# Experts with weights split ahead of time into float32r parts in DRAM, in two slots of one expert each

## The chip, the cores and the metric

The kernel runs on one core of a Trainium2 chip. The metric is the device time of one execution in microseconds (us), the median of several runs. The core has five engines that run their own instruction streams and wait for each other by semaphores: TensorE (PE; weight loads are listed as PEld), VectorE (DVE), ScalarE (ACT), GpSimd (POOL) and SyncE (SP), which here only issues transfers.

## What is computed

Two blocks of a graph network and a mixture of experts each, on 3125 nodes of 256 features and 50000 edges. The change is in the first mixture of experts (16 experts, the best two for each row), whose weights it prepares during the graph part ahead of it:

```python
x = x + L0_gnn(layernorm(x), weight[16], edge_weight, src, dst, edge_type)
x = x + L0_ffn(layernorm(x), ...)
# L0_ffn: D_MODEL 256, HIDDEN 512, 16 experts
probs = softmax(x @ gate_w + gate_b);  top_probs, top_idx = top_k(probs, 2)
hidden = silu(x @ w1[e]) * (x @ w2[e])      # 256 -> 512, for each chosen expert e
out = sum over the two chosen e of (hidden @ w3[e]) * share[e]      # 512 -> 256
x = x + L1_gnn(layernorm(x), ...);  x = x + L1_ffn(layernorm(x), ...)
```

All is float32. float32r is a form in which TensorE takes a float32 matrix product in one pass with fewer bits; a product kept near float32 is made of three such terms (high x high, high x low, low x high), where low is what the rounding to high left over.

## The kernel before

The stages run one after another, with a barrier of four engines between them.

**Transform** (lines 404 to 450). All nodes times the 16 relations' matrices: 25 row tiles, each 8 groups of six float32r products of 512 columns (L422). ScalarE copies each group's bank to the stage buffer (L434), SyncE writes it to DRAM (L439). VectorE splits the tile's rows into high and low parts, and at chosen tiles builds edge tables (`dve_tables`).

**Gather** (lines 722 to 845). 196 blocks of 256 edges. GpSimd fetches the transformed rows with 392 indirect loads (L784); before the blocks b = 8, 12, ... it waits until block b-5 has landed (`ld_ok`). TensorE multiplies each of 221 steps with a one-hot matrix from VectorE (L826) and VectorE adds the result (L835). Beside it ScalarE makes 28 pairs of one-hot tables for later (`act_places`, L740 to L755), each written to DRAM.

**Routing** (`*_routing`): norm, gate logits, the best two experts, the place of each row in a list sorted by expert. An expert has whole tiles of 128 rows; MT = 64 tiles is the most that can occur and all 64 are run. VectorE ends the routing with the place tables (`fri`, `toi`) and then with work on the next layer's weights (L1066 to L1072).

**Experts' stage** (`*_moe`), the place of the change, a loop over 64 tiles:
- SyncE (`sp_tile`) loads the three matrices of the tile's expert, 512 KB each, for every tile, into one of three buffers. The expert's number is in a register of SyncE.
- GpSimd (`rows_of_tile`) fetches the tile's 128 rows, and scatters the results (`results`).
- TensorE (`pe_moe`): turns the rows of tile j+1 (L1255, L1256), makes the two up products of tile j in plain float32 with the weights stationary (L1267; 16 products of 128x128, two instructions each), so that the hidden rows come out transposed, and the down product of tile j-1 as three float32r terms (L1279, 12 products of 256 columns).
- ScalarE copies the turned rows (L1297), rounds w3 (L1304), applies Silu (L1308), rounds the hidden rows (L1310). VectorE makes w3's low part (L1323), Silu times the second up product (L1326), the hidden rows' low part (L1328), and copies out (L1335).

The engines' order is the order of the code; there is no planner. Addresses of weights in SBUF are constants, chosen by j % 3.

## Time and profile before

| | us |
|---|---|
| median of 3 runs | 2679.85 (2675.83 to 2681.54) |
| the profiled execution | 2671.94 |
| its span | 2670.2 |
| transform, first to last product | 30.7 to 309.5 |
| gather, first to last indirect load | 315.3 to 808.8 |
| experts' stage, first up product to last down product | 901.9 to 1237.9 |
| TensorE busy in all | 1939.5 |
| GpSimd busy in all | 1398.1 |

The span is the time between the first and the last instruction of the program. An engine counts as busy while it executes; waits, register steps and the issue of transfers don't count. The end of a matrix product is modelled with its way through the array, so products in a row overlap: their rate is read from start to start. The granted clock of TensorE is given as a share of its full speed.

### The profile page before, as it was taken

To read this page: it belongs to the slowest core of one execution; us is meant where nothing else is said; L and a number is where in the kernel's file an instruction comes from. 1 tells how busy PE (TensorE), PEld (TensorE's weight loads), DVE (VectorE), ACT (ScalarE), POOL (GpSimd) and SP (SyncE) were. 2 spreads that over 40 slices of the span, in tenths; PEclk is the share of its full clock that TensorE was granted. 3 is DMA by queue.
4 is the path that set the end of the run, shared out by engine and by line. 5 is a ranking of instruction groups with operands and counts; after the bars stand their busy time and mean duration, and the time that the engine had idled before them with its cause. 6 is when DMAs were issued, how large, how long until landed. Compare 5 with 4: busy or idle time off the path is not lost.

```text
span 2670.2 us, 37572 instructions
## 1 busy us (share of the span) xinstructions
PE 1939.5 (73%) x10213; PEld 1484.5 (56%) x10213; DVE 1545.9 (58%) x4921; ACT 920.6 (34%) x2031; POOL 1398.1 (52%) x1413
## 2 busy tenths in 40 slices
PE   7999766666666699996466667675466666666798
PEld 5888644444443599996344444444344444444477
DVE  5200134334346755556468787788468787888743
ACT  4444499996002244443221111111311111112522
POOL 1100277777771244432377777771477777772233
PEclk9999878777777799998778788888778888888899
DMA  5544577776334699996455555551455555551000
GB/s 210 201 194 189 200 238 244 237 239 193 105 104 108 229 353 351 352 349 220 155 159 172 158 176 158 172 175 36 141 159 174 157 175 160 170 174 37 1 25 25
DMA packets 206433, 472.17 MB, mean 177 GB/s; under 512 B 33180, under 2 KB 99958, under 8 KB 199762
## 3 DMA queue, kind: packets, MB, share of 16 engines
q0 software_dynamic: 63424, 179.09, 23.3%
q1 hardware_dynamic: 111986, 188.65, 19.8%
q10 hardware_dynamic: 30816, 101.99, 10.7%
q8 instruction: 91, 1.49, 0.2%
q14 instruction: 116, 0.95, 0.1%
HBM read 365.49 MB, written 104.92 MB: 176 GB/s over the span
## 4 chain that ended last, share of the span: by engine, by line
PE 36%; POOL 31%; issue 14%; DVE 11%; DMA 5%; ACT 1%; DVEq 1%; POOLq 0%; SPq 0%; ACTq 0%
POOL arena L1474 18%; POOL arena L784 13%; PE banks L422 10%; PE banks L1267 9%; PE banks L1279 3%; DMA arena<-ht,srcT 3%; PE banks L1583 2%; PE banks L1584 1%; PE banks L1433 1%; DVE arena L1756 1%; PE banks L2175 1%; DVE arena L1672 1%; PE banks L2177 1%; PE banks L2176 1%; DMA arena<-tr,idx1T 1%
## 5 line engine op out<-in xcount | busy, mean ns | idle before, releaser
L1474 POOL DMA_INDIRECT arena<-ht,srcT x784 | 785.7, 1002 | 311.3 <-issue 231.6
L784 POOL DMA_INDIRECT arena<-tr,idx1T x392 | 375.3, 957 | 327.1 <-DMA tr<-arena 207.9
L812 PE MATMUL banks<-arena 128*128 x884 | 323.6, 522 | 182.5 <-SPq L791 170.8
L1583 PE MATMUL banks<-arena,XT 128*128 128x264 f32 x884 | 375.8, 515 | 103.0 <-DVE arena L1756 84.9
L812 PEld LDWEIGHTS banks<-arena 128*128 128x128 f32 x884 | 213.8, 259 | 292.3 <-issue 258.4
L1584 PE MATMUL banks<-arena,XT 128*128 128x264 f32 x884 | 335.3, 468 | 0.0
L1756 DVE TENSOR_TENSOR arena<-arena,nrmT 128x528 f32<-128x528 f32 x442 | 309.6, 703 | 20.3 <-ACT nrmT L1530 19.0
L1583 PEld LDWEIGHTS banks<-arena,XT 128*128 128x128 f32 x884 | 188.6, 241 | 201.1 <-DVE arena L1756 133.5
L422 PE MATMUL banks<-parts 128*128 128x512 f32 x1200 | 275.0, 391 | 4.7 <-DVE parts L382 4.7
L835 DVE TENSOR_TENSOR X<-X,banks 128x256 f32 x221 | 91.9, 416 | 312.4 <-PE banks L812 311.6
L422 PEld LDWEIGHTS banks<-parts 128*128 128x128 f32 x1200 | 226.0, 189 | 52.3 <-issue 5.3
L1510 ACT COPY xn<-arena 128x16 f32 x448 | 54.5, 202 | 554.9 <-SPq L791 547.5
L1584 PEld LDWEIGHTS banks<-arena,XT 128*128 128x128 f32 x884 | 213.4, 241 | 51.3
L1267 PE MATMUL banks<-arena 128*128 128x128 f32 x2048 | 240.4, 275 | 0.0
L1267 PEld LDWEIGHTS banks<-arena 128*128 128x128 f32 x2048 | 235.0, 193 | 0.0
L1541 PE MATMUL banks<-ident,xn 128*64 128x128 f32 x112 | 31.2, 375 | 269.3 <-ACT xn L1510 269.3
L1672 DVE TENSOR_TENSOR arena<-arena,banks 128x264 f32 x442 | 188.7, 427 | 13.2 <-PE banks L1584 3.2
L434 ACT COPY arena<-banks 128x512 f32<-128x512 f32 x200 | 116.8, 587 | 160.1 <-PE banks L422 155.1
L1541 PEld LDWEIGHTS banks<-ident,xn 128*64 128x64 f32 x112 | 9.6, 130 | 291.3 <-ACT xn L1510 237.0
L1156 POOL DMA_INDIRECT ys<-arena x64 | 63.9, 999 | 185.6 <-DVE arena L1335 185.6
L826 DVE TENSOR_SCALAR arena<-iorow,dlT,nrmT 128x128 f32<-128x128 f32 x442 | 137.6, 362 | 31.8 <-PE banks L422 31.8
L751 ACT ACTIVATE arena<-iorow,dlT 128x128 bf16<-128x128 f32 x448 | 133.8, 387 | 11.3 <-ACT arena L742 11.3
(370 smaller groups left out, 3033.2 us busy)
## 6 DMA issues: line engine op xcount, KB each, us to landing
arena<-in_L_ffn_w_dram SPq DMA_DIRECT2D x192, 512.0 KB, 6.1
tr<-arena SPq DMA_DIRECT2D x50, 1024.0 KB, 3.9
XT<-otd ACTq DMA_DIRECT2D x52, 512.0 KB, 4.5
...
arena<-ht,srcT POOLq DMA_INDIRECT x784, 2.9
```

The costliest lines, as they stand in the source:

```text
L422: mm = ten.matmul(B[b][:, :], x[c][:, k, :], w[:, k, 2 * j:2 * j + 2, :].rearrange("p r d -> p (r d)"), start=(n == 0), stop=(n == 5))
L434: act.copy(stage[:, i % 2, j * 512:(j + 1) * 512], B[j % 6][:, :]).then_inc(ev_ok, 1)
L751: v = ac.put(act.activation(OHs[b][:, j * P:(j + 1) * P], iorow[:, :], ACT.Abs, scale=-1.0, bias=dlT[:, q:q + 1]))
L784: pool.indirect_dma_start(Gr[:, o:o + D], None, TR, bass.IndirectOffsetOnAxis(ap=idx1T[:, q:q + 1], axis=0)).then_inc(d_g[b % NG], 16)
L812: mm = ten.matmul(B[n][:, 0:D], OHr[:, n, h, :], Gr[:, h * D:][:, bass.ds(o, D)], start=(h == 0), stop=(h == 1))
L826: vec.tensor_scalar(OHr[:, n, h, :], iorow[:, :], dlT[:, q:q + 1], nrmT[:, q:q + 1], ALU.is_equal, ALU.mult).then_inc(oh_r, 1)
L1267: mm = ten.matmul(B[bank][:, h * P:(h + 1) * P], W[b][:, k, h * P:(h + 1) * P], xTt[c][:, k, :], start=(k == 0), stop=(k == 1))
L1474: pool.indirect_dma_start(Gall[:, o:o + ROW], None, HT[L], bass.IndirectOffsetOnAxis(ap=srcT[:, q:q + 1], axis=0)).then_inc(d_g[b % NG], 16)
L1583: ten.matmul(B[n][:, 0:MSG], OH[b][:, 2 * j, :], WG[:, j, 0, :], start=True, stop=False)
L1584: mm = ten.matmul(B[n][:, 0:MSG], OH[b][:, 2 * j + 1, :], WG[:, j, 1, :], start=False, stop=True)
L1672: ins = vec.tensor_tensor(o, o, B[j % 4][:, 0:MSG], ALU.add)
L1756: vec.tensor_tensor(WG[:, j].rearrange("p a (h c) -> p a h c", c=HW), gm, ex.to_broadcast([P, 2, 8, HW]), ALU.mult).then_inc(w_ok, 1 + CH ...
```

## The change

- **Splitting.** A DRAM tensor WS holds, for each expert and each of its three matrices, the high and the low part side by side, 1 MB a matrix. 48 pieces (one matrix each) are read by ScalarE's queue, rounded by ScalarE, subtracted by VectorE and written back by ScalarE's queue: `act_piece` 15 times at the end of a row tile of the transform and once in each of the 28 iterations of `act_places`, the rest behind it; `dve_piece` in step with it, in the gather at fixed steps (`low_at`).
- **Slots.** Two slots in SBUF of one expert each (three matrices, high and low, 3 MB). SyncE loads expert 0 at the start of the routing, expert 1 when the places are known, and expert e into slot e % 2 matrix by matrix as soon as the last tile of expert e-2 has used that matrix. Every expert is loaded once, in the order of their numbers.
- **Up products.** Now with the turned rows stationary and the weights moving: six float32r products of 512 columns for each of w1 and w2 (three terms, two halves of the depth). The hidden rows come out by row, so TensorE transposes them (four transposes), and ScalarE and VectorE take high and low from the bank. The turned rows are split too (L1393, L1425). w3 is no longer rounded in the loop.
- **Registers.** A tile's slot and what its matrices must have reached are read by TensorE from two tables, eight tiles at a time (`pe_slot`), and each product's address is computed from a register.
- **Routing.** VectorE no longer makes the experts' numbers ahead of the place tables; behind `fri` it makes the three tables of slot, turn and first tile.

The diff, cut to its core:

```diff
+        def act_piece(q):
+            b, c = q % 2, 1 - q % 2
+            if q == 0:
+                act.wait_ge(d_dl, 64)
+                act.wait_ge(tb_ok, 5)
+            if q > 1:
+                e, m = divmod(q - 2, 3)
+                act.wait_ge(wl_ok, LOW0 + q - 1)
+                act.dma_start(WS[e, :, m * 2 * PIECE:(m + 1) * 2 * PIECE], pieces[b]).then_inc(d_ps[b], 16)
+            if q < PIECES:
+                e, m = divmod(q, 3)
+                act.dma_start(praw[b].rearrange("p (k h) -> p k h", k=(2, 2, 4)[m]), wv[m][e]).then_inc(d_pr[b], 16)
+            if 0 < q <= PIECES:
+                act.wait_ge(d_pr[c], PR0 + 16 * ((q - 1) // 2 + 1))
+                if q > 2:
+                    act.wait_ge(d_ps[c], PS0[c] + 16 * ((q - 3) // 2 + 1))
+                act.copy(phi[c], praw[c]).then_inc(wh_ok, 1)
+        def dve_piece(q):
+            b = q % 2
+            vec.wait_ge(wh_ok, HIGH0 + q + 1)
+            vec.tensor_tensor(plo[b], praw[b], phi[b].bitcast(F32), ALU.subtract).then_inc(wl_ok, 1)
...
             for i in range(NT):
                 act_rows(i)
+                if BEGIN <= i < BEGIN + EARLY:
+                    act_piece(i - BEGIN)
 
...
                 act.dma_start(OHD[c], OHs[b]).then_inc(d_oe[b], 16)
+                act_piece(EARLY + c)
+            for q in range(EARLY + NCH, PIECES + 2):
+                act_piece(q)
+            for b in range(2):
+                act.wait_ge(d_ps[b], PS0[b] + 16 * (PIECES // 2))
...
+        low_at = {13 * (c + 1) // 2 + 8: EARLY + c - 1 for c in range(NCH)}
+        low_at.update({13 * NCH // 2 + 8 + 3 * n: EARLY + NCH + n - 2 for n in range(1, PIECES + 2 - EARLY - NCH)})
...
+                if s in low_at:
+                    dve_piece(low_at[s])
...
+            vec.wait_ge(er_ok, 1)
+            vec.tensor_scalar(turn_e[0:1, :], B[5][0:1, 0:MT], 16.0, None, ALU.mult).then_inc(ej_ok, 1)
+            ex, pr = exf[0:1, :], pairf[0:1, :]
+            step(vec.tensor_scalar(ex, B[5][0:1, 0:MT], -1.0, None, ALU.add))
+            step(vec.tensor_scalar(pr, ex, 0.5, -0.25, ALU.mult, ALU.add))
+            step(vec.tensor_scalar(pr, pr, WHOLE, None, ALU.add))
+            step(vec.tensor_scalar(pr, pr, -WHOLE, None, ALU.add))
+            step(vec.scalar_tensor_tensor(pr, pr, -2.0, ex, ALU.mult, ALU.add))
+            vec.tensor_scalar(slot_e[0:1, :], pr, float(SLOT), None, ALU.mult).then_inc(ej_ok, 1)
+            vec.tensor_copy(used[0:1, :], ts_[0:1, :]).then_inc(ej_ok, 1)
...
+            sync.wait_ge(d_zg, 48)
+            for m in range(3):
+                sp_matrix(0, m)
...
+        def sp_matrix(e, m):
+            o = slice(m * 2 * PIECE, (m + 1) * 2 * PIECE)
+            if e:
+                sync.wait_ge(d_ew[m], 16 * e)
+            sync.dma_start(of_slot[e % 2][:, o], WS[e, :, o]).then_inc(d_ew[m], 16)
 
         def sp_moe():
-            sync.wait_ge(ej_ok, 2)
-            for j in range(NW):
-                if j == NW - 1:
-                    sync.wait_ge(fr_ok, 1)
-                sp_tile(j)
-            for j in range(NW, MT):
-                sp_tile(j)
+            sync.wait_ge(fr_ok, 1)
+            for m in range(3):
+                sp_matrix(1, m)
+            sync.wait_ge(ej_ok, 3)
+            sync.load(ru, used[0:1, 0:R])
+            for e in range(2, R):
+                sync.reg_alu(ahead_, ru[e - 1], 1, ALU.max)
+                for m, done in enumerate((u1_ok, u2_ok, dn_ok)):
+                    sync.wait_ge(done, ahead_)
+                    sp_matrix(e, m)
...
+        def pe_slot(j):
+            k, i = (j // CH) % 2, j % CH
+            if i == 0:
+                ten.load(rp[k], slot_e[0:1, j:j + CH])
+                ten.load(rw[k], turn_e[0:1, j:j + CH])
+        def slot_of(j, m):
+            ten.reg_alu(landed, rw[(j // CH) % 2][j % CH], 16, ALU.max)
+            ten.wait_ge(d_ew[m], landed)
+            return ten.snap(rp[(j // CH) % 2][j % CH], min_val=0, max_val=SLOT)
+        def pe_up(j, m, done):
+            c = j % 2
+            o = slot_of(j, m)
+            terms = [(x, k, w) for x, w in ((xth, 0), (xth, 1), (xtl, 0)) for k in range(2)]
+            for n, (x, k, w) in enumerate(terms):
+                mm = ten.matmul(B[2 * m + c][:, :], x[c][:, k * P:(k + 1) * P],
+                                slots[:, (2 * m + w) * PIECE + k * HID:][:, bass.ds(o, HID)], start=(n == 0), stop=(n == 5))
+            mm.then_inc(done, 1)
+        def pe_first(j):
+            ten.wait_ge(tl_ok, j + 1)
+            pe_slot(j)
+            if j > 1:
+                ten.wait_ge(hl_ok, j - 1)
+            pe_up(j, 0, u1_ok)
+        def pe_second(j):
+            if j > 1:
+                ten.wait_ge(hd_ok, j - 1)
+            pe_up(j, 1, u2_ok)
+        def pe_turn_hidden(j):
+            c = j % 2
+            ten.wait_ge(hd_ok, j + 1)
+            for h in range(4):
+                tr = ten.transpose(B[c][:, h * P:(h + 1) * P], hid[c][:, h * P:(h + 1) * P], ident[:, :])
+            tr.then_inc(ht_ok, 1)
 
         def pe_down(j):
             c = j % 2
             ten.wait_ge(hl_ok, j + 1)
-            ten.wait_ge(w3_ok, j + 1)
             if j > 1:
                 ten.wait_ge(yo_ok, j - 1)
-            terms = [(x, w, h) for x, w in ((hidh, w3h), (hidh, w3l), (hidl, w3h)) for h in range(4)]
+            o = slot_of(j, 2)
+            terms = [(x, w, h) for x, w in ((hidh, 0), (hidh, 1), (hidl, 0)) for h in range(4)]
             for n, (x, w, h) in enumerate(terms):
-                mm = ten.matmul(B[4 + c][:, 0:D], x[c][:, h * P:(h + 1) * P], w[c][:, h, :], start=(n == 0), stop=(n == 11))
+                mm = ten.matmul(B[4 + c][:, 0:D], x[c][:, h * P:(h + 1) * P],
+                                slots[:, (4 + w) * PIECE + h * D:][:, bass.ds(o, D)], start=(n == 0), stop=(n == 11))
             mm.then_inc(dn_ok, 1)
 
         def pe_moe():
+            ten.wait_ge(ej_ok, 3)
             pe_turn_rows(0)
             for j in range(MT):
+                pe_first(j)
+                if j:
+                    pe_turn_hidden(j - 1)
                 if j + 1 < MT:
                     pe_turn_rows(j + 1)
-                pe_up(j)
+                pe_second(j)
                 if j:
                     pe_down(j - 1)
+            pe_turn_hidden(MT - 1)
             pe_down(MT - 1)
 
...
             if j > 1:
                 act.wait_ge(u2_ok, j - 1)
-            act.copy(xTt[c], B[6 + c][:, 0:2 * P].rearrange("p (k c) -> p k c", k=2)).then_inc(tc_ok, 1)
+            act.copy(xth[c], B[6 + c][:, 0:2 * P]).then_inc(th_ok, 1)
 
         def act_up(j):
-            b, c = j % NW, j % 2
-            act.wait_ge(d_ew[b], 48 * (j // NW + 1))
-            if j > 1:
-                act.wait_ge(dn_ok, j - 1)
-            act.copy(w3h[c], W3[b]).then_inc(w3h_ok, 1)
+            c = j % 2
             act.wait_ge(u1_ok, j + 1)
             if j > 1:
                 act.wait_ge(hd_ok, j - 1)
             act.activation(sil[c], B[c][:, :], ACT.Silu).then_inc(si_ok, 1)
-            act.wait_ge(hd_ok, j + 1)
-            act.copy(hidh[c], hid[c]).then_inc(hh_ok, 1)
+        def act_hidden(j):
+            c = j % 2
+            act.wait_ge(ht_ok, j + 1)
+            if j > 1:
+                act.wait_ge(dn_ok, j - 1)
+            act.copy(hidh[c], B[c][:, :]).then_inc(hh_ok, 1)
 
         def act_moe():
             act.wait_ge(d_xs, 16 * NGR)
             act_turned_rows(0)
             for j in range(MT):
+                act_up(j)
+                if j:
+                    act_hidden(j - 1)
                 if j + 1 < MT:
                     act_turned_rows(j + 1)
-                act_up(j)
+            act_hidden(MT - 1)
+        def dve_turned_rows(j):
+            c = j % 2
+            vec.wait_ge(th_ok, j + 1)
+            if j > 1:
+                vec.wait_ge(u2_ok, j - 1)
+            vec.tensor_tensor(xtl[c], B[6 + c][:, 0:2 * P], xth[c].bitcast(F32), ALU.subtract).then_inc(tl_ok, 1)
 
         def dve_up(j):
-            b, c = j % NW, j % 2
-            vec.wait_ge(w3h_ok, j + 1)
-            vec.tensor_tensor(w3l[c], W3[b], w3h[c].bitcast(F32), ALU.subtract).then_inc(w3_ok, 1)
+            c = j % 2
             vec.wait_ge(u2_ok, j + 1)
             vec.wait_ge(si_ok, j + 1)
+            if j > 1:
+                vec.wait_ge(ht_ok, j - 1)
             vec.tensor_tensor(hid[c], sil[c], B[2 + c][:, :], ALU.mult).then_inc(hd_ok, 1)
+        def dve_hidden(j):
+            c = j % 2
             vec.wait_ge(hh_ok, j + 1)
-            vec.tensor_tensor(hidl[c], hid[c], hidh[c].bitcast(F32), ALU.subtract).then_inc(hl_ok, 1)
+            if j > 1:
+                vec.wait_ge(dn_ok, j - 1)
+            vec.tensor_tensor(hidl[c], B[c][:, :], hidh[c].bitcast(F32), ALU.subtract).then_inc(hl_ok, 1)
 
...
+            dve_turned_rows(0)
             for j in range(MT):
+                if j:
+                    dve_hidden(j - 1)
+                if j + 1 < MT:
+                    dve_turned_rows(j + 1)
                 dve_up(j)
                 if j:
                     dve_down(j - 1)
+            dve_hidden(MT - 1)
```

What this does to TensorE's order, first before: one tile in the steady part of the experts' stage. `tc_ok` is ScalarE's copy of the turned rows, `d_xg` and `d_ew` are loads of rows and weights, `si_ok` and `hd_ok` are Silu and the product of the two halves, `hl_ok` the hidden rows' low part, `yo_ok` the copy of the result. A float32 product is one row here and two instructions in the trace.

```order
L1255 MATMUL banks<-ident,arena 128x128 [waits tc_ok,d_xg1]
L1256 MATMUL banks<-ident,arena 128x128
L1267 MATMUL banks<-arena 128x128 [waits si_ok,tc_ok,d_ew0]
L1267 MATMUL banks<-arena 128x128 x7
L1267 MATMUL banks<-arena 128x128 [waits hd_ok]
L1267 MATMUL banks<-arena 128x128 x7
L1279 MATMUL banks<-parts 128x256 [waits yo_ok,w3_ok,hl_ok]
L1279 MATMUL banks<-parts 128x256 x11
```

After, the same place, from the turning of tile j-1's hidden rows to the first steps of tile j's second up product (`tl_ok` is the low part of the turned rows).

```order
L1358 MATMUL banks<-ident,arena 128x128 [waits hd_ok]
L1358 MATMUL banks<-ident,arena 128x128 x3
L1320 MATMUL banks<-ident,arena 128x128 [waits tl_ok,d_xg0]
L1321 MATMUL banks<-ident,arena 128x128
L1329 REGISTER_ALU [waits hd_ok]
L1331 ISA [waits d_ew1]
L1338 MATMUL banks<-parts 128x512
L1338 ISA
L1338 MATMUL banks<-parts 128x512
L1338 ISA
```

Four transposes stand where there were none, and the product's first two steps are register steps, one of them with the wait for the matrix. From the end of that up product to the start of the down product of tile j-1. ISA is the step that computes an address from a register.

```order
L1338 MATMUL banks<-parts 128x512 x3
L1329 REGISTER_ALU [waits hl_ok]
L1331 ISA [waits d_ew2]
L1369 MATMUL banks<-parts 128x256
L1369 ISA
L1369 MATMUL banks<-parts 128x256
L1369 ISA
```

The down product, one row of twelve products before, now has a register step with the wait for `hl_ok` ahead of it and seven more between its first eight products; turned hidden rows and the second up product stand ahead of it.

TensorE at every eighth tile, from the last rows of the down product, after:

```order
L1369 MATMUL banks<-parts 128x256 x5
L1326 TENSOR_LOAD arena [waits tl_ok]
L1327 TENSOR_LOAD arena
L1329 REGISTER_ALU [waits hl_ok]
L1331 ISA [waits d_ew0]
L1338 MATMUL banks<-parts 128x512
L1338 ISA
```

Two loads of registers from SBUF stand between the down product and the next first up product; before there was no such load in the stage.

ScalarE, one tile in the steady part, before:

```order
L1297 COPY arena<-banks 128x256 [waits u2_ok,tn_ok]
L1304 CAST parts<-arena 128x1024 [waits dn_ok,d_ew1]
L1308 ACTIVATE arena<-banks 128x512 [waits hd_ok,u1_ok]
L1310 CAST parts<-arena 128x512 [waits hd_ok]
L1297 COPY arena<-banks 128x256 [waits u2_ok,tn_ok]
```

and after:

```order
L1400 ACTIVATE arena<-banks 128x512 [waits hd_ok,u1_ok]
L1407 CAST parts<-banks 128x512 [waits dn_ok,ht_ok]
L1393 CAST parts<-banks 128x256 [waits u2_ok,tn_ok]
L1400 ACTIVATE arena<-banks 128x512 [waits hd_ok,u1_ok]
```

Its rounding of w3 is gone, and the rounding of the hidden rows (L1310 before, L1407 now) waits for TensorE's transposes (`ht_ok`) and stands between Silu of the next tile and the copy of turned rows.

## Rows read from the trace of the kernel before

**Rows 1.** The page's chain that ended last, shares of the span by engine.
```profile
PE 36%; POOL 31%; issue 14%; DVE 11%; DMA 5%; ACT 1%; DVEq 1%; POOLq 0%; SPq 0%; ACTq 0%
```

**Rows 2.** Windows: us, busy PE, PEld, DVE, ACT, POOL, clock, DMA share, GB/s.
```profile
100.00:310.00 210.00, 209.39 (x932) 172.75 (x930) 23.55 (x68) 88.57 (x152) 4.72 (x4) 1.00 0.47 194
400.00:640.00 240.00, 155.07 (x430) 104.40 (x428) 95.06 (x324) 221.72 (x390) 182.09 (x191) 0.76 0.73 239
...
901.60:1230.70 329.10, 329.10 (x2888) 329.06 (x2888) 185.18 (x254) 160.98 (x253) 126.09 (x121) 1.00 0.99 342
```

**Rows 3.** Chain in order of time: start us, us, what; start and steady part.
```profile
895.55 5.80 DMA arena<-xs,arena
...
1016.72 3.57 PE banks L1267 x32
1020.29 1.43 PE banks L1279 x12
1021.94 3.57 PE banks L1267 x32
```

**Rows 4.** Timeline of one tile: start us, us, engine, line, operation.
```profile
1006.00 0.27 PE L1256 MATMUL banks<-ident,arena 128*128 128x128 f32 x1
...
1006.11 3.74 PE L1267 MATMUL banks<-arena 128*128 128x128 f32 x32
...
1006.58 1.05 ACT L1304 CAST parts<-arena 128x1024 fp32r<-128x1024 f32 x1
...
1007.66 1.23 DVE L1323 TENSOR_TENSOR parts<-arena,parts 128x1024 fp32r<-128x1024 f32 x1 [0.60 <-ACT parts L1304]
1008.09 0.60 ACT L1308 ACTIVATE arena<-banks 128x512 f32<-128x512 f32 x1 [0.47 <-PE banks L1267]
...
1009.60 1.68 PE L1279 MATMUL banks<-parts 128*128 128x256 f32 x12
1009.88 0.69 DVE L1326 TENSOR_TENSOR arena<-arena,banks 128x512 f32<-128x512 f32 x1 [1.00 <-PE banks L1267]
```

**Rows 5.** Chain in order of time, the transform's products.
```profile
124.91 185.04 PE banks L422 x816
```

**Rows 6.** TensorE with registers: timeline of weight loads, and three lines' durations in ns.
```profile
1341.94 0.90 PEld L1552 LDWEIGHTS banks<-arena,XT 128*128 128x128 bf16 x7 [0.84 <-issue]
...
L803 PEldq TENSOR_LOAD <-slot_r x28: 587/592/1309, 310.6 to 802.2; - x28
...
L805 PEldq ALU_OP  x221: 32/33/42, 312.8 to 812.8; - x111
...
L811 PEldq FUSED_REGOPS  x442: 53/53/53, 320.8 to 813.1; - x148
```

**Rows 7.** Timeline, the start of the experts' stage.
```profile
893.16 0.23 DVE L1054 SCALAR_TENSOR_TENSOR arena<-arena 128x64 f32<-128x64 f32 x1
...
901.88 4.92 PE L1267 MATMUL banks<-arena 128*128 128x128 f32 x32
...
902.60 0.48 DVE L1072 MEMSET arena<- 128x512 f32 x1
```

**Rows 8.** GpSimd's indirect loads by line: durations ns min/median/max, first and last start.
```profile
L784 POOL DMA_INDIRECT arena<-tr,idx1T x392: 949/953/1065, 315.3 to 808.8; - x196
...
DMA to landing us min/median/max: 2.7/3.3/5.3
...
L1151 POOL DMA_INDIRECT arena<-xs,arena x64: 952/1107/1181, 894.3 to 1212.3; - x64
...
DMA to landing us min/median/max: 2.7/6.5/7.8
```

**Rows 9.** DMA queues in 920:1230, then 100:310: packets, MB, share of 16 engines.
```profile
q1 hardware_dynamic: 63084, 91.91, 85.2%
...
q1 hardware_dynamic: 5984, 40.19, 46.3%
```

**Rows 10.** ScalarE's issues of the tables' writes by line, first and last start.
```profile
L755 ACTq DMA_DIRECT2D ohd<-arena x28: 326/326/327, 330.2 to 644.9; - x28
```

81 lines of the change are left out of this document (38 added, 43 removed).

## Prediction

> **What bounds the kernel now.** I read the chain that ended last first [rows 1]: 36% of the span is TensorE, 31% GpSimd. The stretches [rows 2] say where. In the transform (100 to 310 us shown) TensorE is never idle. In the gather GpSimd issues 392 indirect loads one behind another, from 315.3 to 808.8, a start every 1.26 us [rows 8] while ScalarE builds tables beside it until 645 [rows 10]. In the experts' stage (901.6 to 1230.7) TensorE is busy for every one of 329.1 us at the full clock, and DMA is busy too, 0.99. The chain of that stage in order of time [rows 3] shows a tile as 3.57 us of up products (16 float32 products, 32 instructions), 1.43 us of down products, 0.22 us of turning, and the next tile starts 5.22 us after the last: no wait in it. So the change acts on the path only in the experts' stage; its preparation lands beside TensorE (transform) and beside GpSimd (gather), where it costs nothing unless it disturbs them.
>
> **Part 1, TensorE's own work per tile.** Out go 3.57 us. In come twelve float32r products of 512 columns; the transform runs that form, 816 in 185.04 us, 0.227 each [rows 5], so 2 x 1.36 = 2.72 us. The gate's hidden rows now come out by row, so four transposes are added; a transpose of that form starts 0.11 us behind the last L1256 to L1267 [rows 4], 0.43 us. Down stays 1.43, turning 0.22. Sum 4.80 us against 5.22: 0.42 x 63 = 26.5 us less, if TensorE still never waited.
> The Trainium skill (TensorE: Matmul & The Clock Gate, Back-to-back issue gap) gives about 131 ns for a product of 512 columns in a stream with weight loads. By it the up products would take 1.57 us and the stage save some 70 us more; [rows 5] have 227 ns for this form, and the measurement decides.
>
> **Part 2, a new chain inside a tile.** Before, TensorE had a tile's 3.57 us of up products to run while VectorE and ScalarE made the hidden rows of the tile before, and no down product of the steady stage waits. Now TensorE runs: first up product (j), turn hidden (j-1), turn rows (j+1), second up product (j), down (j-1). Down waits for the low part of the turned hidden rows, and ScalarE must do Silu (j) before it may copy hidden (j-1). From the end of the first up product: 0.20 us until ScalarE starts (the 16th of L1267's products ends at 1006.11 + 1.79 = 1007.90, Silu starts at 1008.09), Silu 0.60, the high part 0.60 (same shape as Silu, also from a bank), 0.03 to VectorE, low part 0.69 from a bank (L1326), all [rows 4]. ScalarE's two steps overlap by some 0.1 us, so the signal is there after 2.02 us. TensorE has 0.43 + 0.22 + 1.36 = 2.01 us of work in that time, so the signal alone would cost nothing. But the down product no longer stands ready in the queue.
>
> **Part 3, registers in TensorE's stream.** The weights' address now comes from a register. A product whose address is computed just ahead of it starts 0.13 us behind the last one: seven weight loads in 0.90 us, (0.90 - 0.10) / 6 [rows 6]. For up products of 0.227 us that hides. Of the twelve down products (0.119 each) eight have such a step, and since the wait stands ahead of a register step, nothing of them is issued before the signal. From signal to first product I estimate 0.03 (as from ScalarE to VectorE) + 0.09 (the step of 33 ns and 0.06 behind it) + 0.10 (the step of 53 ns and 0.05), out of the 0.13 that a step and its product take: 0.23 us, so the wait is 0.24 us. Down itself: 8 x 0.131 + 4 x 0.119 = 1.52, 0.09 more. Behind it the next first product needs two more such steps and an extra wait; I estimate 0.1 us of gap. A tile: 4.80 + 0.24 + 0.09 + 0.10 = 5.23 us, against 5.22. The whole gain of part 1 is given back: 0 us, with bounds of -21 (only the 0.09 is paid: 4.89 us) and +12 (each of the three hand-overs 0.06 us dearer).
> **Loads of the registers.** Every eighth tile TensorE's sequencer loads two tables of eight registers, 0.59 us each [rows 6], 1.25 together, behind the down products' issue, which itself runs live (part 3). Issue of down ends at most 0.15 us ahead of its execution, so some 1.2 us show. Seven times: +8.4 us. Bounds: 0 (all hidden) and 9.
>
> **Part 4, start and end of the stage.** The first up product stood at 901.88, behind a row load of 5.8 us. VectorE was busy with the next layer's weights until 903.08 [rows 7]. Now it has to make the low part of tile 0's rows first, and it comes behind that work and behind seven more small steps of 0.23 us or less (the place of an expert's slot). 903.1 + 1.5 + 0.4 = 905.0, then the two register loads 1.25 and 0.23: 906.5. That is +4.6 us. At the end the last tile has transposes and the high part from a bank in its tail: 0.43 + 0.20 + 0.60 + 0.03 + 0.69 + 0.23 = 2.2 us stand behind the last but one's down product. Before it was 2.3 us from the last up product (0.20 + 0.69 + 0.03 + 0.60 + 0.03 + 0.69 + 0.06) less that down product's 1.43, 0.9 us: +1.3 us.
>
> **Part 5, the weights' DMA in the stage.** Before: 1.5 MB for each of 64 tiles. Now 3 MB for each of 16 experts, which with the reference's inputs have 3 3 8 3 5 5 3 2 4 3 3 4 5 2 4 2 tiles of rows (59, and 5 empty ones). A slot is refilled during the expert between; the smallest such stretch is two tiles plus the 3.5 us of slack from one matrix's last use to its next, 14 us. At the cost per MB of these 2 KB packets (85.2% of 310 us for 91.91 MB [rows 9], 2.87 us) 3 MB take 8.6 us, plus under 3 for rows. No wait: 0 us. DMA was at 0.99 but TensorE never waited for it, so relief gives nothing either.
>
> **Part 6, splitting the weights: 48 pieces.** In the transform ScalarE has 15 of them, each a copy of 1024 columns (1.05 us) and two issues of 0.33. It evicts eight banks, some 0.6 us each, in 10.9 us (185.04 / 17 rows), and TensorE has six banks in turn, 6.8 us of slack against a delay of 2 us: 0 us. In the gather 28 iterations of 11.7 us [rows 10] become 13.5 or are paced by VectorE, which takes the low parts at fixed steps, the last at step 208 of 221, about 763 us by the loads' pace; ScalarE is done near 770, and the last load is issued at 808.8: 0 us, with 40 us in hand. DMA: a piece reads 0.5 MB and writes 1 MB, 1.4 + 2.4 us of all engines (46.3% of 210 us for 40.19 MB of 8 KB rows, [rows 9]). Per 14.5 us that is 0.27 on top of 0.73 [rows 2], so 1.0 at the worst. GpSimd may issue eight loads beyond one that has not landed, 10 us; they land in 3.3 [rows 8], and in the experts' stage with DMA at 0.99 the same shape landed within 7.8. So no stall. VectorE's low parts overlap GpSimd's issue: L784 takes 0.953, L1151, beside a subtraction of the same kind, 1.107 [rows 8]. 34 of them x 0.15 = 5 us at most; I take +2 (bounds 0 and 5).
>
> **Sum.** 0 + 8.4 + 4.6 + 1.3 + 2 = +16.3, less 0.3 for a small step that the routing no longer has ahead of its tail: +16. On the profiled execution's 2671.94 us this gives 2688. That execution is 7.9 us under the median of the runs, which I carry over: 2679.85 + 16 = 2696.
>
> **Rivals.**
> (a) TensorE hardly waits: the queue takes the down product at once and the loads fall into its run-ahead. 4.89 us a tile, -21, + 4.6 + 1.3 + 2 - 0.3 = -13, 2667; with the loads still paid, 2675. For it: before, TensorE shows no wait in the whole stage [rows 2, 3]. Against: the order puts the wait ahead of a register step, and the chain of part 2 is as long as its cover.
> (b) About even: half of part 3's wait and half of the loads, 2680 to 2685.
> (c) The gather's DMA saturates. With 8 KB packets beside the 1 KB rows a load lands in 12 us, not 3.3; it decides from 10 us on. Each group of eight then costs 2 us; 44 groups: +88, some 2784.
> (d) VectorE's subtraction shuts GpSimd out of its descriptors for as long as it runs: 34 pieces in the gather x 1.23 (the form of L1323) = +42 us, 2738. By [rows 8] L1151 loses 0.15 us beside such an operation, not 1.2, so it gets little.
> The Trainium skill (SBUF — State Buffer, SBUF: two separate sides) states such an exclusive lock, for a VectorE operation with two SBUF inputs against a GpSimd operation that reads SBUF; that speaks for (d).
> (e) Refills come late. It decides where 3 MB take over 14 us instead of 8.6: at 20 us the two stretches of two tiles each wait 6 us and the five of three tiles 1 us each, +17 on the forecast, 2713.
>
> **Chances.** Forecast with its own range 2685.5 to 2710: 0.50. (a) 0.18, (b) 0.17, (c) 0.05, (d) 0.04, (e) 0.06. The range 2668 to 2720 leaves out the better half of (a), (c) and (d). About 0.2% (5.4 us) is what a measurement can tell here: faster 0.18 (a), same 0.17 (b), slower 0.65 (the rest). It ends slower in the forecast and in (c) to (e), faster in (a).
>
> **What would show it.** In the changed kernel's chain: a tile's period (5.23, or 4.89 by (a)); idle time of TensorE ahead of the down products, put down to VectorE's low part (0.2 to 0.35 us); a gap of 1.2 us at every eighth tile; the first up product near 906.5. GpSimd's 392 loads still 1.26 us apart, and the last of them near 809. I am wrong if the period is under 5.1, or if the end of the gather moves by more than 5 us.

## The result, and the profile after

The changed kernel takes 2742.55 us (median of 4 runs, 2739.09 to 2751.73) against 2678.02 (4 runs) of the kernel before: 1.0245 times, 95% interval 1.0217 to 1.0273. It is slower, as forecast, but by 64.5 us and not by 16; 2742.55 lies above the range of 2668 to 2720. The profiled execution has a span of 2740.1 us where the one before has 2670.2, so the traces have 69.9 us to explain.

Page of the changed kernel, its head:

```profile
span 2740.1 us, 36576 instructions
...
PE 1944.0 (71%) x9189; PEld 1436.4 (52%) x9189; DVE 1541.9 (56%) x4975; ACT 890.6 (33%) x2015; POOL 1404.2 (51%) x1413
```

Read along the stages, by the starts and ends of the same work in both timelines:

| | before | after | difference |
|---|---|---|---|
| first indirect load of the gather | 315.3 | 316.0 | +0.7 |
| last one starts | 808.8 | 823.8 | +15.0 in all |
| last step of the rows' places (`fri`) starts | 893.8 | 908.9 | +15.1 |
| first up product | 901.9 | 924.1 | +22.2 |
| last down product ends | 1238.15 | 1304.14 | +66.0 |
| end of the span | 2670.2 | 2740.1 | +69.9 |

So the gather costs 15 (0.7 of it is its later start), the start of the tiles 7 and the tiles 44. The last 4 come from stages with the same program in both kernels: what lies behind the last down product took 1432.0 before and 1436.0 after, and 1436.0 in a second profile of the kernel before, so they are no cost of the change.

**The tiles.** Chain in order of time, around an eighth tile (start, duration, what; "issue" is time in which the engine waited for nothing that the profile shows). L1338 is an up product's six matmuls, L1358 the four transposes of hidden rows, L1320 and L1321 those of rows, L1369 the down product:

```profile
959.82 1.77 PE banks L1369 x12
961.59 1.40 PE banks L1338 x6
962.98 0.44 PE banks L1358 x4
...
963.64 1.38 PE banks L1338 x6
965.06 1.86 PE banks L1369 x12
966.92 3.51 issue
970.43 2.44 PE banks L1338 x6
972.88 0.85 PE banks L1358 x4
973.73 0.21 PE banks L1320
973.95 0.21 PE banks L1321
974.16 1.57 PE banks L1338 x6
975.73 1.42 PE banks L1369 x12
```

From one down product to the next are 5.24 us (959.82 to 965.06), next to 5.22 before the change [rows 3], and 5.23 was forecast. Behind the eighth tile stand 3.51 us of "issue", and then every matmul takes about twice its time (four transposes 0.85 for 0.44). The granted clock is 0.50 from 971 to 974.4 us, the lower of its two levels (1.2 GHz). The next gap stands at 1013.86: eight tiles take 46.9 us instead of 41.9, and later ones up to 48.2. Seven of these make up about 40 of the 44 us. At the gap TensorE's sequencer loads its registers, two lines of eight words each; durations in ns, min/median/max:

```profile
L1326 PEldq TENSOR_LOAD <-arena x8: 1931/1937/1950, 919.9 to 1251.6; - x8
...
L1327 PEldq TENSOR_LOAD <-arena x8: 1943/2119/2350, 921.9 to 1253.6; - x8
```

The same instruction with as many words takes 0.59 us in the gather [rows 6]; I had put that in. The stretches (busy us of PE, PEld, DVE, ACT, POOL, granted clock, DMA share, GB/s) show TensorE idle for 8% of the time, and a mean clock below 1.00. It was 1.00 before, with no idle time [rows 2].

```profile
1000.00:1100.00 100.00, 92.37 (x511) 76.26 (x509) 35.06 (x68) 23.00 (x52) 33.26 (x34) 0.95 0.53 184
1100.00:1200.00 100.00, 91.89 (x506) 75.74 (x505) 35.00 (x68) 22.98 (x51) 32.42 (x34) 0.93 0.60 211
```

The Trainium skill (Runtime: NRT & Kernel Launch, Instruction fetch mechanics) puts a load of registers from HBM at about 200 ns each even in bulk; as an estimate, eight would take 1.6 us by it. The tables here lie in SBUF, so no run shows the page's case: these two lines have 240 to 290 ns for each register and [rows 6] have 74. The experiments say what separates the two.

**The gather.** GpSimd's issues and one of VectorE's low parts beside them:

```profile
388.61 1.84 POOL L834 DMA_INDIRECT arena<-tr,idx1T  x1 [0.30 <-issue]
...
388.41 1.22 DVE L704 TENSOR_TENSOR parts<-arena,parts 128x1024 fp32r<-128x1024 f32 x1
...
664.59 0.95 POOL L834 DMA_INDIRECT arena<-tr,idx1T  x1 [0.31 <-issue]
665.85 1.39 POOL L834 DMA_INDIRECT arena<-tr,idx1T  x1 [0.30 <-issue]
...
665.19 1.22 DVE L704 TENSOR_TENSOR parts<-arena,parts 128x1024 fp32r<-128x1024 f32 x1
```

L704 is the subtraction of a piece (34 in the gather). 60 of the 392 issues overlap one; they take 1197 ns on average, the other 332 take 957. 60 x 0.24 = 14.4 us. That is the stage's loss: between its issues GpSimd is idle for 119.2 us in all in both kernels, and the issues themselves take 389.6 us instead of 375.3. The issues wait 0.9 us in all for transfers.

The average hides what happens. The issue at 388.61 begins 0.2 us after a subtraction has begun and ends 0.82 us after its end (390.45 against 389.63); the one at 665.85 does the same (667.24 against 666.41). The one at 664.59 was 0.6 us under way when the subtraction began, and lost nothing. It is so throughout: 25 issues that found a subtraction under way, and of it more than 0.13 us to come, end 0.82 to 0.83 us after its end and lose 14.5 us together; the other 35 lose 0.1 us together. An issue is held at one point, about 0.13 us behind its start, until the subtraction is over.

**The start.** Timeline, from the last steps of VectorE's work for the graph stages to the first up product:

```profile
909.36 0.96 POOL L1213 DMA_INDIRECT arena<-xs,arena  x1 [75.98 <-DVE arena L1109]
...
916.71 0.42 PE L1321 MATMUL banks<-ident,arena 128*128 128x128 f32 x1
...
919.10 0.48 DVE L1134 MEMSET arena<- 128x512 f32 x1
919.51 0.35 DVE L1425 TENSOR_TENSOR parts<-banks,parts 128x256 fp32r<-128x256 f32 x1
924.11 2.92 PE L1338 MATMUL banks<-parts 128*128 x6 [6.97 <-issue]
```

The first tile's rows were turned at 917.1; their low part (L1425) ran at 919.5, behind VectorE's other work, and then both register loads came in front of the product. From the first load of rows to the first up product are 14.75 us; it was 7.6 before.

### The profile page after: what moved, and what is told of

Read it like the earlier page. It is cut to its first block, busy times and chain, and to the rows that moved or that the text cites. A ratio compares the mean times of both kernels' runs of the same rounds, so it can differ in the third digit from the quotient of the medians.

```text
span 2740.1 us, 36576 instructions
## 1 busy us (share of the span) xinstructions
PE 1944.0 (71%) x9189; PEld 1436.4 (52%) x9189; DVE 1541.9 (56%) x4975; ACT 890.6 (33%) x2015; POOL 1404.2 (51%) x1413
## 4 chain that ended last, share of the span: by engine, by line
PE 36%; POOL 29%; issue 15%; DVE 13%; DMA 4%; DVEq 1%; ACT 1%; POOLq 0%; SPq 0%; ACTq 0%
POOL arena L1592 15%; POOL arena L834 13%; PE banks L431 10%; PE banks L1338 7%; PE banks L1369 4%; DMA arena<-ht,srcT 3%; PE banks L1701 2%; PE banks L1702 2%; DVE arena L1874 2%; PE banks L1551 1%; DVE arena L1790 1%; PE banks L1358 1%; PE banks L2293 1%; DMA arena<-tr,idx1T 1%; PE banks L2295 1%
## 5 line engine op out<-in xcount | busy, mean ns | idle before, releaser
L834 POOL DMA_INDIRECT arena<-tr,idx1T x392 | 389.6, 994 | 327.1 <-DMA tr<-arena 207.9
L1701 PE MATMUL banks<-arena,XT 128*128 128x264 f32 x884 | 370.1, 508 | 104.7 <-DVE arena L1874 84.8
L862 PEld LDWEIGHTS banks<-arena 128*128 128x128 f32 x884 | 218.3, 262 | 302.0 <-issue 266.4
L1702 PE MATMUL banks<-arena,XT 128*128 128x264 f32 x884 | 333.6, 466 | 0.0
L1701 PEld LDWEIGHTS banks<-arena,XT 128*128 128x128 f32 x884 | 183.9, 236 | 205.1 <-DVE arena L1874 138.2
L431 PEld LDWEIGHTS banks<-parts 128*128 128x128 f32 x1200 | 226.8, 189 | 52.3 <-issue 5.1
L1338 PE MATMUL banks<-parts 128*128 x768 | 218.9, 423 | 32.2 <-issue 28.4
L1702 PEld LDWEIGHTS banks<-arena,XT 128*128 128x128 f32 x884 | 210.4, 238 | 49.3
L1790 DVE TENSOR_TENSOR arena<-arena,banks 128x264 f32 x442 | 188.5, 426 | 14.4 <-PE banks L1702 4.0
L1338 PEld LDWEIGHTS banks<-parts 128*128 128x128 f32 x768 | 145.3, 202 | 58.8 <-issue 34.0
L1213 POOL DMA_INDIRECT arena<-xs,arena x64 | 62.4, 975 | 168.9 <-PE banks L1321 90.2
L1440 DVE TENSOR_TENSOR parts<-banks,parts 128x512 fp32r<-128x512 f32 x64 | 44.2, 691 | 167.8 <-ACT parts L1407 167.8
```

What stands on the lines that cost most here:

```text
L431: mm = ten.matmul(B[b][:, :], x[c][:, k, :], w[:, k, 2 * j:2 * j + 2, :].rearrange("p r d -> p (r d)"), start=(n == 0), stop=(n == 5))
L834: pool.indirect_dma_start(Gr[:, o:o + D], None, TR, bass.IndirectOffsetOnAxis(ap=idx1T[:, q:q + 1], axis=0)).then_inc(d_g[b % NG], 16)
L862: mm = ten.matmul(B[n][:, 0:D], OHr[:, n, h, :], Gr[:, h * D:][:, bass.ds(o, D)], start=(h == 0), stop=(h == 1))
L1338: mm = ten.matmul(B[2 * m + c][:, :], x[c][:, k * P:(k + 1) * P], slots[:, (2 * m + w) * PIECE + k * HID:][:, bass.ds(o, HID)], start=(n = ...
L1701: ten.matmul(B[n][:, 0:MSG], OH[b][:, 2 * j, :], WG[:, j, 0, :], start=True, stop=False)
L1702: mm = ten.matmul(B[n][:, 0:MSG], OH[b][:, 2 * j + 1, :], WG[:, j, 1, :], start=False, stop=True)
```

## Experiments

Four kinds of question: what the register loads cost and why, what a tile consists of, what disturbs the gather, what stands in the start. The kernel before took 3163 to 3194 us on the three chips on which most of the runs were made, and 2678 on the chip of before_again, g5_five and d2_beside, as on that of the first measurement. On the three, pauses of 2 to 8 us, in which no engine has an instruction under way, lengthen the gather and the graph stages. The tiles are alike on both (380 us in the changed kernel), so I compare stages within a group of runs, and ratios with the kernel before on the same chip. "Tiles" means from the first up product's start to the last down product's end: 336.3 us before, 380.0 after.

### The tables from which registers are loaded

```
-  used, slot_e, turn_e = take(R, dt=I32), take(MT, dt=I32), take(MT, dt=I32)
+  used = take(R, dt=I32)
+  slot_e, turn_e = slot_r[:, 0:MT], slot_r[:, 64:64 + MT]
```

> Edit: the two tables from which TensorE's sequencer loads eight registers at a time (slot_e, turn_e) stand in slot_r, dead by then, at its words 0 and 64, instead of at words 11661 and 11725 of the arena; nothing else changes. In the changed kernel the two loads took 1.93 to 2.35 us, and every eighth tile began 3.5 us late and then ran its matmuls at half clock (46.9 to 47.8 us for eight tiles against 8 x 5.24 = 41.9). Theory A (the words' place is the cost: slot_r's were loaded in 0.59 us in the gather): loads of 0.59 us, gap of about 0.8 us, clock stays up, about -4 us in each of seven groups and -2.7 us at the start: 2742 - 30 = 2712. Theory B (it is the transfers of the weights that run beside them, or the stage, not the place): loads of 1.9 to 2.4 us as before, time within 3 us of 2742.

The other kernel of this pair has `slot_r[:, 13:13 + MT], slot_r[:, 85:85 + MT]`.

> Edit: as a1_low, but at words 13 and 85 of slot_r, so that no group of eight words begins at a multiple of 32 bytes, as in the arena. Theory A1 (a start off the 32-byte grid is the cost): loads of 1.9 us again, time about 2742. Theory A2 (the arena, its address or its being written by other engines, is the cost): loads of 0.59 us, time as a1_low, about 2712. Theory B: 1.9 to 2.4 us and 2742 in both.

The loads of a1_low, then of a2_mis:

```profile
L1327 PEldq TENSOR_LOAD <-slot_r x8: 587/590/592, 985.2 to 1286.6; - x8
L1328 PEldq TENSOR_LOAD <-slot_r x8: 587/588/589, 985.9 to 1287.3; - x8
```

```profile
L1327 PEldq TENSOR_LOAD <-slot_r x8: 1932/1934/1957, 981.6 to 1311.6; - x8
L1328 PEldq TENSOR_LOAD <-slot_r x8: 1944/2109/2477, 983.6 to 1313.6; - x8
```

a1_low: 3171.18 us, 1.0027 times the kernel before (1.0013 to 1.0040), tiles 347.4 us, 32.6 less than in the changed kernel (28 was expected). a2_mis: 3205.43, 1.0146 (1.0123 to 1.0169), tiles 377.8. Moving the tables by 13 and 21 words costs 34 us. Theory A1 holds: what counts is where the eight words begin. On a multiple of 32 bytes they are loaded in 0.59 us. In the arena the tables began at words 11661 and 11725, which like 13 and 85 lie five words past such a multiple; whether a start on 16 or 8 bytes would do was not tried. The gap in a1_low's chain, as it should have been by the forecast:

```profile
1071.18 1.73 PE banks L1370 x12
1072.91 0.69 issue
1073.60 1.65 PE banks L1339 x6
1075.25 0.44 PE banks L1359 x4
```

0.69 and a first up product 0.25 longer, and the granted clock stays at 1.00. Next, early loads, with the tables where they were:

```
   pe_second(j)
+  if j % CH > CH - 3:
+      pe_slot(j + 2)        # one table for each call, not both at j % CH == 0
   if j:
       pe_down(j - 1)
```

> Edit: the tables stay in the arena; each load is issued earlier and apart from the other, the first behind the second up product of the tile whose number is 6 modulo 8, the other behind that of the tile 7 modulo 8, and the first group's two ahead of the first transposes. If TensorE's queue held enough work to hide 1.95 us, the gaps of 3.5 us would go altogether: -5 us x 7 = -35, and 2707. Against that: in the changed kernel the first load began about 1.0 us after the down product's first matmul of 1.75 us, so that only some 0.75 us of work was queued ahead of it; then each load opens a gap of 1.95 - 0.75 = 1.2 us, less the 0.24 us that TensorE waits there anyway, so about 2 us for a group instead of 3.5, and the clock stays up since no gap is long: -3 us x 7 = -21 and about -2 at the start: 2719. I take the second.

3165.47 us, 1.0005 (0.9991 to 1.0019), tiles 339.6 us: 40.4 us less, twice what I took, though the loads still take 1.93 to 2.39 us. The first load of one group started at 1016.12, 1.34 us before the second up product in front of it (1017.46), since the sequencer had run ahead of the engine; it ended at 1018.41, and the queued work lasted until 1018.85, 2.7 us from the load's start. I had read the depth of the queue from the down product, which is issued live, and that is the one place where there is none. Both remedies together, `top[0] += -(top[0] + 23040) % 8` ahead of the tables:

> Edit: the two tables stay in the arena but begin at a multiple of eight words (32 bytes), and each load is issued on its own, ahead of the tile that needs it (as a3_early). So far: the tables on the 32-byte grid of slot_r were loaded in 0.59 us and the stage from the first up product to the last down product took 347.5 us (379.9 in the changed kernel), off the grid in slot_r 1.93 us and 377.7 us; the early loads in the arena, though still 1.93 to 2.39 us long, gave 339.6 us. If the grid alone counts: 0.59 us here too; then the stage is that of early loads or better, 64 tiles x 5.24 = 335 to 339.6 us, and the time as a3_early or up to 4 us less, 1.000 of before on this chip. If the arena counts: loads of 1.93 us and 339.6 us.

3162.34 us, 1.0005 (0.9989 to 1.0020), tiles 338.1. The loads of c1_grid_early:

```profile
L1328 PEldq TENSOR_LOAD <-arena x8: 588/592/596, 979.2 to 1271.2; - x8
```

The arena itself costs nothing; words off the grid of 32 bytes do. One more run was to load the four kinds of place in turn on GpSimd:

> Edit: the changed kernel with one load of eight registers by GpSimd's sequencer behind the results of each tile, from four places in turn: words 16 and 21 of slot_r (on and off the 32-byte grid), words 11664 and 11669 of the arena (on and off it). The registers are not used. Theory A1: about 0.6 us on the grid and 1.9 us off it, in both buffers. A2: 0.6 us from slot_r, 1.9 us from the arena, on the grid or off. B: all four alike, 1.9 us. The time itself stays at 2742 (GpSimd waits over half of each tile).

Its trace has none of those loads (presumably dropped, since nothing used their registers), so it tells nothing of them (3210.91 us, tiles 379.9, as the changed kernel). And the changed kernel itself on these chips:

> Edit: none, the changed kernel as it is, since the chips of the runs so far gave the kernel before 3163 to 3165 us where the first chip gave 2678. The stage of the expert tiles was alike on both (379.9 us), so the change costs the same there; the gather and the graph stages behind are longer here, by pauses of 2 to 8 us, so that the gather's end hangs less on GpSimd. If so: 1.0245 of before in the first runs, here 64.5 us less the gather's 15, on 3164: about +50, 3214 us, ratio 1.016. If all is stretched alike: 1.0245, 3240 us.

3249.48 us, 1.0173 (1.0154 to 1.0192), tiles 379.7: the tiles' cost is the same. The whole is 55 us above the kernel before on this chip, near the +50 (1.016) of the first forecast and away from the 1.0245 of the second.

### What a tile consists of

```
-  ten.reg_alu(landed, rw[(j // CH) % 2][j % CH], 16, ALU.max)
-  ten.wait_ge(d_ew[m], landed)
-  return ten.snap(rp[(j // CH) % 2][j % CH], min_val=0, max_val=SLOT)
+  e = expert_of[j]
+  ten.wait_ge(d_ew[m], 16 * (e + 1))
+  return (e % 2) * SLOT
```

> Edit: the changed kernel, in its order, with no register in TensorE's expert tiles: the slot and the count of landed matrices of each tile are written in as constants, as this input gives them, and both table loads and all address computations are gone. Theory (step 3 of the prediction): the tile's 5.24 us holds about 0.3 us of TensorE idle before the down product, since its sequencer computes three registers after the wait; without them 64 tiles at 4.95 to 5.05 us, no gaps and full clock: stage 317 to 323 us. Rival: the toll is the wait for the hidden rows alone and registers add nothing: stage 335 us, as with the early loads (c1_grid_early, 338 us).

The chain of f1_fixed:

```profile
1022.99 1.53 PE banks L1366 x12
1024.52 1.39 PE banks L1336 x6
...
1026.57 1.39 PE banks L1336 x6
1027.96 1.53 PE banks L1366 x12
```

4.97 us a tile and 321.6 for all, inside the forecast. So registers are 0.27 us of a tile's 5.24. Most of it lies in the down product itself: twelve matmuls take 1.53 us here and 1.72 to 1.88 in the changed kernel. The next kernel keeps the registers (grid and early loads as c1_grid_early) and moves the down product:

```
   pe_second(j)
-  if j:
-      pe_down(j - 1)
+  if j > 1:
+      pe_down(j - 2)
```

> Edit: c1_grid_early, and each down product stands one tile later in TensorE's program (behind the second up product of tile j comes the down product of tile j - 2, not j - 1), its eviction on VectorE too. Theory (step 3 of the prediction): the tile of 5.23 us is 4.8 us of TensorE's work and 0.4 us in which its sequencer had to wait for the hidden rows' low part and so started the down product with an empty queue (twelve matmuls in 1.72 to 1.88 us; 1.42 where the queue was full). With a tile's distance the wait is over long before: tile 4.80 us, stage 64 x 4.8 = 307 to 312 us, -27 us against c1_grid_early. Rival: registers and address computations are the toll, a tile stays at 5.1 to 5.24 us and the time within 8 us of c1_grid_early. Another: with the tile shorter, an expert's weights come late (3.1 MB for each expert), and some tiles wait on the DMA: tile between.

Its chain and one of its stretches:

```profile
1025.04 1.40 PE banks L1371 x12
1026.44 1.38 PE banks L1341 x6
1029.85 1.40 PE banks L1371 x12
...
1100.00:1200.00 100.00, 100.00 (x627) 89.02 (x625) 42.68 (x84) 28.37 (x63) 40.72 (x42) 1.00 0.71 245
```

4.81 us a tile, the down product in 1.40 with all its registers, TensorE never idle: tiles 310.9 us, 27 less than in c1_grid_early. 3132.35 us, 0.9909 of the kernel before (0.9879 to 0.9938). The rival, that registers are a toll wherever they stand, is out: with work queued ahead they cost nothing. Nor do weights come late at 4.81 us a tile.

### What disturbs the gather

```
-  vec.tensor_tensor(plo[b], praw[b], phi[b].bitcast(F32), ALU.subtract).then_inc(wl_ok, 1)
+  w = slice(0, PIECE if q < EARLY - 2 else 1)
+  vec.tensor_tensor(plo[b][:, w], praw[b][:, w], phi[b][:, w].bitcast(F32), ALU.subtract).then_inc(wl_ok, 1)
```

> Edit: the changed kernel with the low part's subtraction on VectorE cut to one column for the pieces that fall into the gather (34 of them; their low parts are left out, all transfers and ScalarE's copies stay). Theory L (VectorE's read of two operands from SBUF shuts out GpSimd, which writes descriptors: the 60 indirect DMA issues beside a subtraction took 1197 ns instead of 957, 14.4 us in all): the last issue of the gather begins about 14 us earlier than in c1_grid_early of this call. Rival: on this chip the gather's end came at 877 to 881 us against 825 in the first trace, so that its DMAs, not GpSimd, set its end; then it ends within 3 us of c1_grid_early.

In g2_oneinput the line is `vec.tensor_scalar(plo[b], praw[b], 0.0, None, ALU.mult)`, in g3_quarters four subtractions of 256 columns.

> Edit: the changed kernel with the subtraction replaced, in the gather, by a multiplication of the raw piece by a number: the same 1024 columns read and written by VectorE, with one operand from SBUF (the low parts come out wrong). Theory L, the form in which two operands are what shuts GpSimd out: no issue of GpSimd beside it is longer than 957 ns on average, and the gather ends as in g1_onecol. If any long operation of VectorE does it, or the transfers do: as in c1_grid_early. VectorE's own time, one operand instead of two, is about half of 1.22 us at least.

> Edit: the changed kernel with each subtraction of the gather issued as four of 256 columns instead of one of 1024. Measured so far: 34 subtractions of 1.22 us lengthened GpSimd's issues by 20.8 us in all on these chips (17.6 on the first), multiplications of 0.69 us by 12.3, one column by 2.7. If an issue waits until the running VectorE operation ends, and slips in between two: less than half of it is left, under 10 us, and no issue is longer than 1.4 us. If GpSimd's and VectorE's accesses only share a port in proportion: 17 to 22 us as before, the longest near 2.0.

GpSimd's issues in g1_onecol and g2_oneinput, and VectorE's operation in g2_oneinput and g3_quarters:

```profile
L835 POOL DMA_INDIRECT arena<-tr,idx1T x391: 947/953/1061, 316.2 to 877.3; - x196
```

```profile
L837 POOL DMA_INDIRECT arena<-tr,idx1T x392: 949/957/1472, 316.4 to 877.6; - x196
...
L707 DVE TENSOR_SCALAR parts<-arena x34: 678/685/694, 363.0 to 882.3; 128x1024 fp32r<-128x1024 f32 x34
```

```profile
L709 DVE TENSOR_TENSOR parts<-arena,parts x136: 410/417/481, 369.9 to 886.4; 128x256 fp32r<-128x256 f32 x136
```

The excess of the 392 issues over the shortest form (0.949 each), summed:

| VectorE beside the gather | its time, us | issues' excess, us | of it above 3 |
|---|---|---|---|
| nothing (kernel before) | 0 | 3 | 0 |
| 34 x one column (g1) | 5 | 3 | 0 |
| 34 x one operand, 1024 (g2) | 23.3 | 12.3 | 9 |
| 34 x two operands, 1024 (c1, a1, changed kernel) | 41.5 | 18 to 23 | 15 to 20 |
| 136 x two operands, 256 (g3) | 56.7 | 19.0 | 16 |

With all transfers and ScalarE's copies in place but hardly any subtraction, the excess is gone: it is VectorE's access. The form of theory L in which only two operands hold GpSimd up fails, since one operand does too. The single issues say how. In g2_oneinput those that begin under the multiplication again end 0.82 to 0.83 us after it; others, 0.22 to 0.49 us under way when it began, end 0.12 us after it, so there is a second point at which this operation holds an issue, and the subtraction doesn't. In g3_quarters each held issue ends 0.83 us after the end of a quarter, some after that of the first, some (2.2 us long) after that of the last: neither forecast, to slip in between the quarters or to share in proportion, describes that. The Trainium skill (SBUF — State Buffer, SBUF: two separate sides) states an exclusive lock between GpSimd and a VectorE operation with two SBUF inputs, or one in a 2-port mode, for the whole instruction. The traces agree for VectorE's operation, behind which an issue waits until its end; an issue holds nothing for its whole length, since subtractions that begin 0.08 to 0.95 us into one take their 1.22 us. Whether the multiplication ran in such a mode, no trace names.

On the slower chips the end of the gather did not follow (the last issue starts at 875 to 883 us in all of them, g1_onecol's 877.3 against 875.0 in c1_grid_early, as its rival had it). In every one of these runs GpSimd stood still 11 to 17 times for more than 1 us between two issues, 51 to 75 us in all, and never on a chip of the first kind; so the time had to be tested elsewhere.

> Edit: none, the kernel before, for its trace on these chips. In the first trace the gather's last issue began at 808.8 us and 92 us later the first up product; the changed kernel's last issue began 15.0 us later. On the chips since then the changed kernel's began at 876 to 884 us. If GpSimd's longer issues (18 to 23 us in all) come through here too: 860 to 866 us. If the pauses of the transfers set the end here: 873 to 881. Stage of the tiles 336 us as on the first chip.

> Edit: the changed kernel with only the first five experts' weights split, all of it in the transform; the other experts' slots are filled from those five, so that the gather holds none of the change's work and the expert tiles compute with wrong weights, in the same time. Expected: gather as in before_again within 3 us, whatever that is; tiles as in the changed kernel, 374 to 380 us. With g1_onecol (the transfers and ScalarE's copies without the subtraction: 876 to 878 us, as with it) this tells what the transfers of 33 pieces (50 MB) cost: the difference between g1_onecol and g5_five. The subtraction's share on these chips is then under 3 us; the transfers' 0 (theory: pauses come anyway) or up to 15.

Both ran on a chip of the first kind (before 2677.63 us, 13 runs), so neither forecast of before_again was put to the test. GpSimd's issues in before_again, then in g5_five:

```profile
L784 POOL DMA_INDIRECT arena<-tr,idx1T x392: 949/953/1081, 315.8 to 808.9; - x196
```

```profile
L835 POOL DMA_INDIRECT arena<-tr,idx1T x392: 949/953/1162, 315.6 to 809.2; - x196
```

Without the change's work the gather ends where it did, 809.2 for 823.8; g5_five takes 2729.32 us (one run), 13 less than the changed kernel. GpSimd's idle time between the issues is 119.2 us in both of these runs, as it was in the changed kernel: transfers cost none of it. That the subtraction makes those 15 us rests on the issues' durations (14.4 us of 15.0, and g1_onecol); there is no run on such a chip with the subtraction alone gone.

### The start, and a version that is no slower

> Edit: b2_lag (tables on the grid, early loads, down product one tile later) with two more: 30 instead of 15 pieces of the weights are split during the transform, two per tile, so that 20 subtractions instead of 34 are left beside the gather; and VectorE's work for the graph stages (10 us that stood between the routing and its first low part of the rows) is spread over the first ten expert tiles. Expected against b2_lag, by stages: from the places of the rows to the first up product -6 us; stage of the tiles as b2_lag, 311 us (VectorE has 2.6 us free in each tile); GpSimd's issues in the gather 8 us shorter in all, of which on these chips some may be lost in pauses; the transform ends later by 0 to 5 us (15 pieces cost it 0.7). Sum: -6 to -14, so 3118 to 3126 on these chips, 0.987 of before. If VectorE bounds the transform with two pieces a tile, +10 us there eats it.

3225.58 us, 1.0091 (1.0072 to 1.0110): a miss. VectorE did not bound the transform; ScalarE waits for a piece's transfers and TensorE for ScalarE, and the gather's first load starts at 371.4 instead of 316. The waits between 150 and 340 us, and a stretch:

```profile
ACT parts L699 <- DMA arena<-in_L_ffn_w_dram: 89.9, 13, 8.5
...
PE banks L431 <- ACT arena L443: 31.4, 12, 3.9
...
200.00:300.00 100.00, 83.42 (x327) 65.26 (x325) 19.70 (x25) 38.83 (x63) 0.00 (x0) 0.91 0.93 354
```

With one piece for each tile the same stretch had a DMA share of 0.91 and TensorE at 100%, so there was little room for more than 15 pieces. So back to 15, with the other edit kept:

```
   dve_down(j - 2)
+  dve_beside(j)      # 1/10 of the steps L1120 to L1134 of the changed kernel
```

> Edit: b2_lag, and VectorE's 10 us of work for the graph stages, which stood between the routing and its first low part of the rows, is spread over the first ten expert tiles (as in d1_all, with one piece for each transform tile, as in the changed kernel). d1_all ended the transform 55 us late, since the transfers of two pieces for each tile (DMA share 0.93) held ScalarE and so TensorE; its tiles took 312 us. Expected here: transform end at 316 us; first up product about 5 us nearer to the places of the rows than in b2_lag (10.6 us in d1_all, 15.2 in the changed kernel); tiles 311 to 313 us; time 5 us under b2_lag: 0.989 of before. If VectorE's extra 1.2 us in each of ten tiles delays the hidden rows: tiles 5 us longer, and no gain.

2671.75 us (10 runs) against 2677.63 (13 runs), 0.9982, interval 0.9964 to 1.0000. In its trace the tiles take 311.8 us and the first up product starts 95.9 us behind the gather's last issue (99.3 in the changed kernel, 92.2 before). Of the 5 us expected at the start against b2_lag only 1.4 came: from the first load of rows to the first up product are 9.3 us, against 10.7 in b2_lag, and now the load of the rows, 7.43 us, is what it waits for. With the tiles 24.5 us shorter than before, the gather's 16 and the start's 4 take most of it back. Against the changed kernel 71 us are won; against the kernel before it is between even and 0.4% faster.

## Why the prediction went wrong in size

- **Part 1 (TensorE's own work, 4.80 us a tile): right.** b2_lag, in which nothing waits, has 4.81.
- **Parts 2 and 3 (a tile): sum right, terms not.** Forecast 5.23, measured 5.24. But the wait of 0.24 ahead of the down product and the gap of 0.1 behind it are not there (0.03 and 0.00). The down product takes 1.72 to 1.88 instead of 1.52, because its matmuls are issued live behind the wait, about 0.15 us each; I had taken 0.131 for eight of them. Registers are 0.27 us of it (f1_fixed), being live the remaining 0.16 (4.97 against 4.81). That the sum fits to 0.01 us is luck.
- **Loads of the registers (+8.4, bounds 0 and 9): the step that failed.** They cost about 40 us (a3_early: 40.4 less). [rows 6] show 0.59 us for a table on a 32-byte grid; the new tables are off it and take 2 us. I took a duration from rows with the same instruction and word count without comparing where the words stand. The trace of the kernel before had a warning: SyncE loads 16 words four times in the experts' stage, from word 11645 of the arena and on, also off the grid, in 3.27 to 3.47 us, and GpSimd in the gather, from a buffer of its own on the grid, in 1.07.

```profile
L1221 SPq TENSOR_LOAD <-arena x4: 3268/3289/3474, 877.8 to 1135.8; - x4
```

A second loss I did not have at all: gaps of 3.5 us are followed by matmuls at half clock, 1.5 to 2.5 us more each time. With loads of 0.59 us the term would have been right: a1_low's tiles are 9.4 us longer than c1_grid_early's, 1.3 for each of seven against 1.2 forecast.
- **Part 4 (start +4.6, tail +1.3).** The start cost 7.1. The mechanism was right, low part behind VectorE's other work, then two loads; the loads of 2 us make the difference. The tail lies within the tiles' sum and was not measured by itself.
- **Part 5 (weights in time): right.** The loads of 1 MB land after 5.2 us (median, 11.4 at most). The profile puts one wait of 3.8 us down to them, ahead of the up product at 1112.60, but that is the fourth of the seven gaps: its second register load took 2.35 us and ended at 1112.33, the product followed 0.27 us behind it, as in the first gap (0.27), and the transfer that the profile names landed at 1113.18, when the product was already running. At 4.81 us a tile (b2_lag) TensorE is never idle.
- **Part 6 (pieces): transform right, gather wrong.** The transform ends 0.7 us later. The gather was given +2, bounds 0 and 5, by L1151's 0.15 us; it cost 15. L1151 had the same subtraction of 1.22 us beside it, but met its last quarter:

```profile
1012.88 1.23 DVE L1323 TENSOR_TENSOR parts<-arena,parts 128x1024 fp32r<-128x1024 f32 x1 [0.60 <-ACT parts L1304]
...
1013.85 1.11 POOL L1151 DMA_INDIRECT arena<-xs,arena  x1 [0.30 <-issue]
```

The subtraction has 0.26 us to go when the issue starts, and the issue ends 0.85 us after it, in 57 of the 64 tiles. In the gather the two meet at any distance: 25 issues are held, for 0.58 us on average and up to 1.05. I took a loss at one fixed distance for the loss of any meeting. Rival (d) had the mechanism, GpSimd shut out until the operation ends, but for its whole length each time, 42 us; a third of it came, since an issue is held at one point only.
- **Rivals.** (c), a gather bound by transfers, did not happen (0.9 us of waits, at a DMA share of 0.92 between 400 and 500 us). (e) neither. (a) was wrong: TensorE's tile is 5.24. 2738 in (d) lies near the result only because two terms that it didn't have happen to make up the same sum.
- **What the parts came to:** gather 15, start 7, tiles 44, together +66 where +16 was forecast.
